# Gates of the expert mixture spread across partitions by DMA, with their chain and the row normalisation moved earlier

## The chip, the cores and the metric

The kernel runs on one core of a Trainium2 chip. The metric is the device time of one execution in microseconds; the number quoted for a kernel is the median of several executions. Engines are named as in the profile: PE is the matrix engine (PEld its weight loads), DVE the vector engine, ACT the scalar engine, POOL the GpSimd engine, and SP issues the DMAs.

## The reference

Three layers run one after the other on x of shape (4, 1024, 256), that is 4096 tokens of width 256, all in float32: a mixture-of-experts feed-forward layer, an attention block with its own small feed-forward, and the same mixture again with the same weights. The change concerns the mixture, which runs twice.

```python
def _L0_ffn_ref(x, gate_W, W1, b1, W2, b2, Ws1, bs1, Ws2, bs2, route_scale):
    scores = sigmoid(x @ gate_W) * route_scale
    topk_scores, topk_idx = top_k(scores, 2)            # 8 experts, 2 chosen
    topk_w = topk_scores / topk_scores.sum(-1, keepdims=True)
    gate_full = einsum('bsk,bske->bse', topk_w, one_hot(topk_idx, 8))
    h = gelu(einsum('bsd,edh->bseh', x, W1) + b1)
    y = einsum('bseh,ehd->bsed', h, W2) + b2
    expert_out = einsum('bse,bsed->bsd', gate_full, y)
    shared = gelu(x @ Ws1 + bs1) @ Ws2 + bs2
    return expert_out + shared

x = x + 0.5 * ffn(layernorm(x))
x = x + attention(layernorm(x))
x = x + 0.5 * ffn(layernorm(x))
```

## The kernel before

`ffn_phase` is the mixture. It is called twice: with tag `f` (first, `tail` set, which also normalises its output twice and transposes it for the attention) and with tag `g` (last, `tail` None). Tiles carry the tag: `f_gbc` and `g_gbc` are the same buffer of the two calls. Between them run `attention_phase` (tag `a`) and `mlp_phase` (tag `m`).

A call works through NB = 8 blocks of BT = 512 tokens. Within a block, `body` runs nine steps e = 0 to 8, one for the shared expert (e = 0) and one for each of the eight experts. All products use a split of each float32 operand into a rounded part and a remainder ("hi" and "lo"), so a product takes three matmuls. In a step PE does: `first_layer` (L855, 6 matmuls of 512 columns into one of two `hid` banks), then `gate` (L873, for e of 1 to 8: one matmul of 512 columns that multiplies a selector `sel` by the stack of transposed gates `gst`, and so leaves the gate of expert e for each token on all 128 partitions, in one of two `gbc` banks), then `second_layer` (L896, 12 matmuls of 256 columns into `acc`) for the step two before, e-2, so that at e = 0 and 1 it still works on the last two steps of the block before. ACT applies GELU (L469) and rounds the gated result to its hi part (L461); DVE multiplies GELU's result by the gate (`gating`, L670, one operand in PSUM) and takes the remainder (`lo`, L676). `second_layer` of step e waits for `lo` of step e; DVE does `lo` of step e during step e+1, right after `gating` of e+1.

Each engine has its own program and works in the order written in its `body`; semaphores tie them. Into the nine steps of block i the code weaves the preparation of block i+1. DVE: `x_stats` (L576, L581; mean and variance) at e = 0, `x_norm` (L594) at e = 1, `xt_lo` (L601) at e = 2, `neg_logits` (L608, L610) at e = 4, `choices` (L627 to L636; the two best experts) at e = 7, `gates` (L643 to L661; their weights, padded in `gpad`) at e = 8. PE: `transposes` (L822) at e = 2, `logits` (L832) at e = 3, and `gates_up` (L842, transposes `gpad`) of block i itself at e = 0 of block i, followed on DVE by `gate_stack` (L665, copies it to `gst`). ACT: `xt_hi` (L442) at e = 2. POOL: `x_rstd` (L536, L538), and `expneg` (L552, a power on 32 elements for each partition). In block 0 of call `f` these are two steps later (`later`). At e = 1 DVE also does `result` (L687) of block i-1. Call `f` adds for block i-1: `z_stats` at e = 3 and `zz_stats` at e = 5 on DVE, `z_rstds` on POOL, `z_norm` and `zn_norm` (L407) on ACT at e = 4 and 7, transposes of `zn` on PE at e = 8, with `zt_hi` (L449) and `zt_lo` (L718); the first and last block of `f` also split the attention's weights (`qkv_lo`, L700) and sum biases (L437, L707) on ACT and DVE.

All these transposes, logits and gates go through the two banks of one PSUM tile, `aux`. SP issues the loads and stores of rows (L330 to L366); `keep_weights` (L302 to L305) stores the split weights for call `g`.

## Time and profile before

| | us |
|---|---|
| median of 3 runs | 2463.55 |
| lowest and highest of them | 2456.26, 2467.4 |
| the profiled execution | 2457.1 |
| its span, first to last instruction | 2454.2 |
| mean granted PE clock, of full speed | 0.996 |

Call `f` takes from 0 to about 287 us of the span, call `g` from about 2196 us to the end. The page of the profile gives the engines' busy time; a busy PE is not PE at its peak, since its matmuls are pipelined and their ends are modelled. How often an engine starts something is therefore read from starts in the timeline, not from durations. "Idle before" is the time in which an engine had nothing running ahead of a group, with the operation whose end released it.

### The profile page before, as it was taken

How to read it: one execution, taken by the hardware profiler on the slowest of the kernel's cores; microseconds unless marked ns; L12 is line 12 of the kernel's file. 1: busy time of each engine (PE TensorE's matmuls, PEld its weight loads, DVE VectorE, ACT ScalarE, POOL GpSimd, SP SyncE). 2: the span in 40 equal slices, each digit the busy share in tenths (PEclk: the TensorE clock that was granted, in tenths of full speed). 3: DMA queues.
4: the chain of work that ended last, by engine and by line, in shares of the span. 5: the costliest groups of instructions: out<-in, count | busy, mean ns of one | idle time of the engine just before them, and what ended most of it. 6: DMA issues, size and time to landing. Idle time of an engine off the chain costs nothing.

```text
span 2454.2 us, 46643 instructions
## 1 busy us (share of the span) xinstructions
PE 2405.0 (98%) x14568; PEld 2087.9 (85%) x14568; DVE 1862.3 (76%) x3599; ACT 1686.6 (69%) x2920; POOL 1505.2 (61%) x1536
## 2 busy tenths in 40 slices
PE   8999889999999999999999999999999999999999
PEld 7888778888888888888888888888888879988888
DVE  7777677878878788887878878788887865556665
ACT  4555577878778787777878778787877864543333
POOL 1333277787777777767777777777768754542220
PEclk9999999999999999999999999999999999999999
DMA  5422531223212132221213312132221345331111
GB/s 204 172 102 94 181 112 44 87 68 96 95 40 89 45 101 71 75 95 43 86 60 100 97 35 94 43 98 73 77 95 43 108 169 171 122 130 34 46 51 43
DMA packets 128311, 220.16 MB, mean 90 GB/s; under 512 B 6810, under 2 KB 89652, under 8 KB 119476
## 3 DMA queue, kind: packets, MB, share of 16 engines
q1 hardware_dynamic: 128180, 218.78, 27.6%
q8 instruction: 37, 0.61, 0.1%
q14 instruction: 94, 0.77, 0.1%
HBM read 114.95 MB, written 53.48 MB: 69 GB/s over the span
## 4 chain that ended last, share of the span: by engine, by line
PE 81%; DVE 8%; issue 6%; POOL 2%; ACT 2%; DMA 1%; SPq 0%; DVEq 0%; ACTq 0%; POOLq 0%
PE a_ov L1622 19%; PE a_sc L1586 18%; PE a_tr L1598 18%; PE a_pj L1541 7%; PE a_pj L1550 4%; PE g_acc L896 3%; PE g_hid L855 3%; PE f_acc L896 3%; PE f_hid L855 2%; PE m_proj L2025 1%; POOL m_zin L1877 1%; PE m_hid L2091 1%; DVE f_hp L676 1%; DVE g_hp L676 1%; PE g_aux L832 1%
## 5 line engine op out<-in xcount | busy, mean ns | idle before, releaser
L1498 DVE TENSOR_REDUCE a_nmax<-a_sc 128x1 f32<-128x1024 f32 x512 | 626.8, 1224 | 260.3 <-PE a_sc L1586 252.1
L1425 POOL TENSOR_SCALAR a_pr<-a_pr,a_rden 128x1024 f32<-128x1024 f32 x512 | 575.1, 1125 | 256.2 <-DVE a_rden L1503 185.7
L1341 ACT ACTIVATE a_pT<-a_tr 128x512 fp32r<-128x512 f32 x1024 | 559.8, 596 | 205.5 <-PE a_tr L1598 197.2
L1509 DVE TENSOR_TENSOR a_pT<-a_tr,a_pT 128x512 fp32r<-128x512 f32 x1024 | 650.1, 677 | 17.7 <-ACT a_pT L1341 17.7
L1622 PE MATMUL a_ov<-a_pT,a_v_s 128*128 128x512 f32 x2048 | 600.2, 415 | 3.1 <-DVE a_half L1489 2.0
L1347 ACT ACTIVATE a_pr<-a_sc,a_nmax 128x1024 f32<-128x1024 f32 x512 | 573.5, 1120 | 31.8 <-DVE a_nmax L1498 28.2
L1586 PE MATMUL a_sc<-a_k_s,a_q_s 128*128 128x512 f32 x2048 | 554.1, 392 | 3.4 <-DMA a_k_s<-a_k_s 3.4
L1598 PEld LDWEIGHTS a_tr<-f_ident,a_pr 128*128 128x128 f32 x4096 | 473.0, 140 | 93.6 <-DVE a_pT L1509 18.8
L1598 PE MATMUL a_tr<-f_ident,a_pr 128*128 128x128 f32 x4096 | 537.8, 273 | 9.8 <-DVE a_pT L1509 9.6
L1586 PEld LDWEIGHTS a_sc<-a_k_s,a_q_s 128*128 128x128 f32 x2048 | 380.0, 188 | 83.7 <-DMA a_k_s<-a_k_s 3.6
L1622 PEld LDWEIGHTS a_ov<-a_pT,a_v_s 128*128 128x128 f32 x2048 | 347.5, 189 | 54.3 <-issue 4.9
L1541 PE MATMUL a_pj<-a_z_s,a_wqk_s 128*128 128x512 f32 x756 | 193.6, 391 | 2.5 <-issue 2.2
L1541 PEld LDWEIGHTS a_pj<-a_z_s,a_wqk_s 128*128 128x128 f32 x756 | 141.6, 188 | 34.9 <-issue 3.3
L1302 ACT ACTIVATE a_staged<-a_pj,f_bias 128x512 f32<-128x512 f32 x126 | 86.8, 689 | 93.8 <-PE a_pj L1541 77.4
L469 ACT ACTIVATE g_act_out<-g_hid,f_b 128x512 f32<-128x512 f32 x72 | 49.6, 688 | 144.5 <-PE g_hid L855 144.5
L896 PEld LDWEIGHTS f_acc<-f_w2p,f_hp 128*128 128x128 f32 x864 | 114.0, 193 | 11.1 <-DVE f_hp L676 6.3
L469 ACT ACTIVATE f_act_out<-f_hid,f_b 128x512 f32<-128x512 f32 x72 | 49.2, 684 | 107.0 <-PE f_hid L855 107.0
L896 PE MATMUL f_acc<-f_w2p,f_hp 128*128 128x256 f32 x864 | 117.5, 286 | 4.5 <-DVE f_hp L676 3.9
L896 PEld LDWEIGHTS g_acc<-g_w2p,g_hp 128*128 128x128 f32 x864 | 112.1, 190 | 8.2 <-DVE g_hp L676 2.9
L896 PE MATMUL g_acc<-g_w2p,g_hp 128*128 128x256 f32 x864 | 115.5, 283 | 1.3 <-DVE g_hp L676 0.9
L855 PE MATMUL f_hid<-f_xT,f_w1p 128*128 128x512 f32 x432 | 115.7, 404 | 0.0
L855 PE MATMUL g_hid<-g_xT,g_w1p 128*128 128x512 f32 x432 | 113.1, 397 | 0.0
(222 smaller groups left out, 3260.0 us busy)
## 6 DMA issues: line engine op xcount, KB each, us to landing
a_z_s<-zT SPq DMA_DIRECT2D x32, 1024.0 KB, 7.8
a_k_s<-a_k_s SPq DMA_DIRECT2D x62, 512.0 KB, 5.7
a_wqk_s<-w_split SPq DMA_DIRECT2D x64, 256.0 KB, 3.2
a_v_s<-a_v_b SPq DMA_DIRECT2D x16, 1024.0 KB, 4.6
att<-a_ao SPq DMA_DIRECT2D x32, 512.0 KB, 2.9
m_in<-att SPq DMA_DIRECT2D x16, 1024.0 KB, 6.1
a_wv_s<-w_split SPq DMA_DIRECT2D x17, 512.0 KB, 3.8
zT<-f_zT SPq DMA_DIRECT2D x8, 1024.0 KB, 3.9
```

What stands on the lines that cost most here:

```text
L469: act.activation(act_out[:, e % 3], hid[:, (par + e) % 2], ACT.Gelu, bias=b1[:, weights_of(e):weights_of(e) + 1]).then_inc(s["gelu"], 1)
L855: o = pe.matmul(hid[:, (par + e) % 2], w1p[:, a, (c * NE + x) * HID:(c * NE + x + 1) * HID], xT[:, par, c, b], start=(n == 0), stop=(n == 5))
L896: o = pe.matmul(acc[:, t], hp[:, e % 3, a, t * P:(t + 1) * P], w2p[:, b, x * D:(x + 1) * D], start=False, stop=(e == NE - 1 and (a, b) == ...
L1341: act.activation(pT[:, (u // 4) % 2, 0, 4 * part:4 * part + 4, (u % 4) * P:(u % 4 + 1) * P], tr[:, part].rearrange("p (t q) -> p t q", t=4 ...
L1347: act.activation(pr[:, k % NP], sc[:, k % 2], ACT.Exp, bias=nmax[:, k % NP:k % NP + 1], accum_out=den[:, k % NP:k % NP + 1]).then_inc(s["e ...
L1425: pool.tensor_scalar(pr[:, k % NP], pr[:, k % NP], rden[:, k % NP:k % NP + 1], 1.0, ALU.mult, ALU.mult).then_inc(s["normed"], 1)
L1498: dve.tensor_reduce(nmax[:, k % NP:k % NP + 1], sc[:, k % 2], AX.X, ALU.max, negate=True).then_inc(s["negmax"], 1)
L1509: dve.tensor_tensor(to[:, 1], tr[:, part].rearrange("p (t q) -> p t q", t=4), to[:, 0].bitcast(F32), ALU.subtract).then_inc(s["tr_lo"], 1)
L1541: o = pe.matmul(bank[:], wqk_s[:, "QK".index(kind), c, a], z_s[:, c * 2 + b, part], start=(i == 0), stop=(i == 5))
L1586: o = pe.matmul(sc[:, k % 2, kb * BT:(kb + 1) * BT], q_s[:, slot, head, tile * P:(tile + 1) * P], k_s[:, slot, head, a, kb * BT:(kb + 1) * ...
L1598: o = pe.transpose(tr[:, part, j * P:(j + 1) * P], pr[:, (k - LAG) % NP, (4 * part + j) * P:(4 * part + j + 1) * P], ident[:])
L1622: o = pe.matmul(ov[:], v_s[:, vslot, kt, 2 * vhead:2 * vhead + 2] .rearrange("p k f -> p (k f)"), pT[:, blk % 2, a, kt], start=(kt == 0 an ...
```

## The change

Blocks 0 and 1 of each call keep the `gate` matmul. For blocks 2 to 7 it is left out. Instead the exact gates are written to a third place of `gpad` (rows 64 to 71 of its transpose), ACT copies these 8 rows of 512 gates from PSUM to `gf` (`gate_copy`), SP stores them to memory (16 KB) and loads them back with one row for all partitions (`gates_across`, two DMAs of four experts each, 1 MB each, into `gB`), and `gating` reads `gB` instead of the PSUM bank. The `gbc` banks, free in these blocks, take the transposes, logits and gates of the next block (`up_bank`); `aux` keeps the `zn` transposes.

The preparation of block i+1 moves within block i to the steps in `STEADY` (before: statistics 0, normalise 1, transposes 2, logits 3, `neg` 4, `choices` 7, `gates` 8, `gates_up` and `gate_stack` at e = 0 of block i+1), and statistics and normalisation are done a block ahead, for block i+2 at e = 6 and 7. `z_stats` moves from e = 3 to 2. On POOL, `expneg` comes before `z_rstds`, and `x_rstd(i + 2)` last. Block 0 has its own schedule, `FIRST`, and does the statistics and normalisation of blocks 1 and 2. Call `f` loads `xin[:, 1]` ahead of the selector and second-layer weights. Several semaphores are merged, here and in the attention and the small feed-forward, with the same order of waits. `body` of `over_blocks` is now written out for blocks 0, 1, 6 and 7.

```diff
+    STEADY = dict(up_x=0, logits=1, neg=2, choices=3, gates=4, up_gates=6, gf=6, stack=6)
+    FIRST = dict(stats=1, norm=2, up_x=3, logits=4, neg=5, choices=7, gates=7, up_gates=8, stack=8) if tail else \
+        dict(stats=0, norm=1, up_x=2, logits=3, neg=4, choices=6, gates=7, up_gates=8, stack=8)
...
+    def on_pe(i):
+        return isinstance(i, int) and i < 2
+    def up_bank(i):
+        return aux if on_pe(i) else gbc
...
+            sp.dma_start(xin[:, 1], rows_of(src, 1)).then_inc(s["sel_in"], 16)
+            sp.wait_ge(s["padded"], 1)
...
+        def gates_across(i, counts):
+            copied, out, used = counts
+            half = E // 2
+            sp.wait_ge(s["gf"], copied)
+            sp.dma_start(gate_rows, gf[EXACT:EXACT + E]).then_inc(s["gates_out"], 16)
+            sp.wait_ge(s["gates_out"], out)
+            for h in range(2):
+                if h == 1:
+                    sp.wait_ge(s["gated"], used)
+                sp.dma_start(gB[:, h * half:(h + 1) * half].rearrange("p e t -> p (e t)"),
+                             gate_rows[h * half:(h + 1) * half].rearrange("e t -> (e t)").unsqueeze(0).partition_broadcast(P))\
+                    .then_inc(s["gates_in%d" % h], 16)
...
+        def gate_copy(i):
+            act.wait_ge(s["gT_ps"], i + 1)
+            if not on_pe(i - 1):
+                act.wait_ge(s["gates_out"], (i - 2) * 16)
+            act.activation(gf[EXACT:EXACT + E], up_bank(i - 1)[EXACT:EXACT + E, 0], ACT.Identity).then_inc(s["gf"], 1)
...
-                if e == 2 + later(first) and not last:
-                    xt_hi(i + 1, 1 - par)
+                if now("up_x", e, first) and not last:
+                    xt_hi(i + 1, 1 - par, up_bank(i))
+                if now("gf", e, first) and not last:
+                    gate_copy(i + 1)
...
-            if not last:
-                x_rstd(i + 1)
-            if tail and not first:
-                z_rstds(i - 1, 0)
+            if first:
+                x_rstd(1)
             if not last:
                 expneg(i + 1)
             if tail and not first:
+                z_rstds(i - 1, 0)
                 z_rstds(i - 1, 1)
+            if has(i, 2):
+                x_rstd(i + 2)
...
+            dve.tensor_copy(gpad[:, :, EXACT:EXACT + E], ga[:])
...
+        def gate_stack(i, par, bank):
+            if on_pe(i):
+                dve.wait_ge(s["gT_ps"], i + 1)
+            else:
+                dve.wait_ge(s["gf"], i - 1)
+            dve.tensor_copy(gst[:, par], bank[:, 0]).then_inc(s["gst"], 1)
         def gating(i, e):
             dve.wait_ge(s["gelu"], i * NE + e + 1)
-            dve.wait_ge(s["gbc"], i * E + e)
-            dve.tensor_tensor(gated[:, e % 3], gbc[:, (e - 1) % 2], act_out[:, e % 3],
-                              ALU.mult).then_inc(s["gated"], 1)
+            if on_pe(i):
+                dve.wait_ge(s["gbc"], i * E + e)
+                gate = gbc[:, (e - 1) % 2]
+            else:
+                dve.wait_ge(s["gates_in%d" % ((e - 1) // (E // 2))], (i - 1) * 16)
+                gate = gB[:, e - 1]
+            dve.tensor_tensor(gated[:, e % 3], gate, act_out[:, e % 3], ALU.mult).then_inc(s["gated"], 1)
...
+                if not last and now("neg", e, first):
+                    neg_logits(i + 1, up_bank(i))
                 if not shared(e):
                     gating(i, e)
                 if e == 1 and not first:
@@ -769,32 +830,37 @@
                     lo(i, e - 1)
                 elif e == 0 and not first:
                     lo(i - 1, NE - 1)
-                if e == 0:
-                    gate_stack(i, par)
+                if e == 0 and first:
+                    gate_stack(0, 0, aux)
                 if tail and first and e == 0:
                     qkv_bias(gbc[:, 1], 1, FIRST_BIAS)
                     w2_low(slice((NE - 1) * D, NE * D))
                 if tail and first and e == 1:
                     w2_low(slice(0, (NE - 1) * D))
                 if not last:
-                    if e == 0 + later(first):
+                    if now("stats", e, first):
                         x_stats(i + 1, 1 - par)
-                    if e == 1 + later(first):
+                    if now("norm", e, first):
                         x_norm(i + 1, 1 - par, False)
-                    if e == 2 + later(first):
-                        xt_lo(i + 1, 1 - par)
-                    if e == 4 + later(first):
-                        neg_logits(i + 1)
+                    if now("up_x", e, first):
+                        xt_lo(i + 1, 1 - par, up_bank(i))
                 if tail and not first:
-                    if e == 3:
+                    if e == 2:
                         z_stats(i - 1)
                     if e == 5:
                         zz_stats(i - 1)
                 if not last:
-                    if e == 7 + later(first) // 2:
+                    if now("choices", e, first):
                         choices(i + 1)
-                    if e == 8:
+                    if now("gates", e, first):
                         gates(i + 1)
+                if has(i, 2):
+                    if e == 6:
+                        x_stats(i + 2, par)
+                    if e == 7:
+                        x_norm(i + 2, par, False)
+                if not last and now("stack", e, first):
+                    gate_stack(i + 1, 1 - par, up_bank(i))
...
-            if shared(e):
+            if shared(e) or not on_pe(i):
...
-                if e == 0 and not first:
-                    if tail:
-                        pe.wait_ge(s["zT_lo"], (i - 1) * DC + 1)
-                    gates_up(i)
                 if not last:
-                    if e == 2 + later(first):
-                        transposes(i + 1, xn, s["xn"], s["xT_ps"])
-                    if e == 3 + later(first):
-                        logits(i + 1, 1 - par)
+                    if now("up_x", e, first):
+                        if not first:
+                            pe.wait_ge(s["gst"], i + 1)
+                        if not on_pe(i):
+                            pe.wait_ge(s["gated"], i * E)
+                            pe.wait_ge(s["gf"], i - 1)
+                        transposes(i + 1, xn, s["xn"], s["xT_ps"], up_bank(i))
+                    if now("logits", e, first):
+                        logits(i + 1, 1 - par, up_bank(i))
+                    if now("up_gates", e, first):
+                        gates_up(i + 1, up_bank(i))
                 if e == 8 and tail and not first:
-                    if not last:
-                        pe.wait_ge(s["neg"], i + 2)
+                    if on_pe(i):
+                        pe.wait_ge(s["gst"], i + 2)
+                        pe.wait_ge(s["gf"], i)
+                    pe.wait_ge(s["zT_lo"], i * DC)
                     transposes(i - 1, zn, s["zn"], s["zT_ps"])
```

## Rows read from the trace of the kernel before

**Rows 1.** Windows, call `f`: us; busy PE, PEld, DVE, ACT, POOL; PEclk, DMA share, GB/s
```profile
146.00:177.00 31.00, 30.79 (x202) 27.70 (x201) 25.24 (x83) 16.07 (x29) 9.00 (x9) 1.00 0.28 101
```

**Rows 2.** Timeline, L888 alone: the four bias matmuls at e = 2 of a block
```profile
L888 PE MATMUL f_acc<-f_b2s,f_gst x4: 278/282/282, 25.0 to 25.3; 128*128 128x256 f32 x4
...
L888 PE MATMUL f_acc<-f_b2s,f_gst x4: 274/280/282, 61.9 to 62.2; 128*128 128x256 f32 x4
...
L888 PE MATMUL f_acc<-f_b2s,f_gst x4: 277/280/354, 158.9 to 159.3; 128*128 128x256 f32 x4
...
L888 PE MATMUL f_acc<-f_b2s,f_gst x4: 278/281/354, 191.4 to 191.8; 128*128 128x256 f32 x4
...
L888 PE MATMUL g_acc<-f_b2s,g_gst x4: 278/281/283, 2298.6 to 2299.0; 128*128 128x256 f32 x4
...
L888 PE MATMUL g_acc<-f_b2s,g_gst x4: 278/281/283, 2330.3 to 2330.6; 128*128 128x256 f32 x4
```

**Rows 3.** Timeline, one step (e = 7) of a block of `g`: start, us, engine, line
```profile
2315.56 1.24 PEld L855 LDWEIGHTS g_hid<-g_xT,g_w1p 128*128 128x128 f32 x6
...
2316.84 0.19 PEld L873 LDWEIGHTS g_gbc<-g_gst,g_sel 128*128 128x128 f32 x1
...
2317.07 1.61 PEld L896 LDWEIGHTS g_acc<-g_w2p,g_hp 128*128 128x128 f32 x12
...
2318.08 0.69 DVE L670 TENSOR_TENSOR g_gated<-g_gbc,g_act_out 128x512 f32<-128x512 f32 x1 [1.76 <-ACT g_act_out L469]
...
2318.61 1.24 PEld L855 LDWEIGHTS g_hid<-g_xT,g_w1p 128*128 128x128 f32 x6
...
2318.68 0.68 DVE L676 TENSOR_TENSOR g_hp<-g_gated,g_hp 128x512 fp32r<-128x512 f32 x1
```

**Rows 4.** Timeline, the same block: start and end of `choices` and `gates`
```profile
2319.28 0.17 DVE L627 TENSOR_SCALAR g_sg<-g_nl 128x32 f32<-128x32 f32 x1
...
2321.64 0.69 DVE L670 TENSOR_TENSOR g_gated<-g_gbc,g_act_out 128x512 f32<-128x512 f32 x1 [0.21 <-DVE g_idx L636]
...
2325.00 0.69 DVE L676 TENSOR_TENSOR g_hp<-g_gated,g_hp 128x512 fp32r<-128x512 f32 x1
...
2325.14 0.42 PEld L842 LDWEIGHTS g_aux<-f_ident,g_gpad 128*128 128x128 f32 x4 [0.59 <-DVE g_gpad L661]
```

**Rows 5.** DVE by line and form, one block of `f`: busy us, mean ns
```profile
L576 DVE BATCH_NORM_STATS2 f_zst<-f_zz 128x6 f32<-128x256 f32 x4 | 1.4, 412 | 0.0
...
L594 DVE TENSOR_SCALAR f_xn<-f_xin,f_mv,f_rs 128x256 f32<-128x256 f32 x4 | 1.4, 406 | 0.0
```

**Rows 6.** Timeline of `f`: POOL operations and the DVE operations beside them
```profile
138.54 5.43 POOL L552 TENSOR_TENSOR f_nl<-f_ebase,f_nl 128x32 f32<-128x32 f32 x1 [1.22 <-DVE f_nl L610]
...
140.82 0.68 DVE L676 TENSOR_TENSOR f_hp<-f_gated,f_hp 128x512 fp32r<-128x512 f32 x1
...
143.85 0.68 DVE L676 TENSOR_TENSOR f_hp<-f_gated,f_hp 128x512 fp32r<-128x512 f32 x1
...
144.05 0.54 POOL L535 TENSOR_SCALAR f_zshift<-f_zmv 128x4 f32<-128x4 f32 x1
```

**Rows 7.** Timeline, ends of blocks 0 and 7 of `f`
```profile
52.78 0.66 PE L842 MATMUL f_aux<-f_ident,f_gpad 128*128 128x128 f32 x4 [1.99 <-DVE f_gpad L661]
...
57.04 2.77 PE L896 MATMUL f_acc<-f_w2p,f_hp 128*128 128x256 f32 x12
...
266.22 2.08 ACT L407 ACTIVATE f_zz<-f_res,f_zshift,f_zrs 128x256 f32<-128x256 f32 x4 [2.01 <-POOL f_zshift L548]
...
271.91 2.38 PE L896 MATMUL f_acc<-f_w2p,f_hp 128*128 128x256 f32 x12 [2.63 <-DVE f_hp L676]
```

**Rows 8.** DMA issues: KB each, median us from issue to landing
```profile
a_z_s<-zT SPq DMA_DIRECT2D x32, 1024.0 KB, 7.8
...
zT<-f_zT SPq DMA_DIRECT2D x8, 1024.0 KB, 3.9
...
f_iota<-in_iota SPq DMA_DIRECT2D x1, 4.0 KB, 2.9
```

More of the change, by code:

```diff
@@ L175, in ffn_phase @@
         b2_in = m.sb("b2_in", [P, D], room=rooms.wide)
-        xres = m.sb("xres", [P, NT, D], room=rooms.rows)
+        xres = m.sb("xres", [P, NT, D], room=rooms.wide)
+        gB = m.sb("gB", [P, E, BT], room=rooms.rows)
+        gf = m.sb("gf", [P, BT], room=Rooms().loads)
         res = m.sb("res", [P, NT, D], room=rooms.tail)
@@ L232, in ffn_phase @@
     names = ("veps x_in xres bn stats rstd xn xT_ps xT_hi xT_lo logits neg expneg "
-             "gate gpad gT_ps gst hid gelu gbc gated h_hi h_lo out res res_out padded")
+             "gate gpad gT_ps gst hid gelu gbc gated h_hi h_lo out res res_out padded "
+             "gf gates_out gates_in0 gates_in1")
     if tail:
-        names += " gate_in w1_in w2_in zeroed gw_hi w1_hi w2_hi sel gw_lo w1_lo w2_lo b2_hi b2_stack kept"
+        names += " gate_in w1_in w2_in gw_hi w_hi rounded gw_lo w_lo b2_stack kept"
         names += " z_veps z_bn z_stats z_rs z_rstd z zn zT_ps zT_hi zT_lo zT_out z_out qkv_in v_in sel_in scaled summed qs qkv_hi qkv_lo qkv_out bias_ps bias"
@@ L258, in ffn_phase, with now, has @@
     SUMS_AT = {4: 0, 6: 1, 7: 2}
-    def later(first):
-        return 2 if tail and first else 0
+    STEADY = dict(up_x=0, logits=1, neg=2, choices=3, gates=4, up_gates=6, gf=6, stack=6)
+    FIRST = dict(stats=1, norm=2, up_x=3, logits=4, neg=5, choices=7, gates=7, up_gates=8, stack=8) if tail else \
+        dict(stats=0, norm=1, up_x=2, logits=3, neg=4, choices=6, gates=7, up_gates=8, stack=8)
+    def now(what, e, first):
+        return (FIRST if first else STEADY).get(what) == e
+    def has(i, ahead=0):
+        return not isinstance(i, int) or 0 <= i + ahead < NB
+    def on_pe(i):
+        return isinstance(i, int) and i < 2
+    def up_bank(i):
+        return aux if on_pe(i) else gbc
     def over_blocks(eng, body):
         body(0, 0, True, False)
-        with eng.Fori(0, (NB - 2) // 2) as it:
-            body(it * 2 + 1, 1, False, False)
+        body(1, 1, False, False)
+        with eng.Fori(0, (NB - 4) // 2) as it:
             body(it * 2 + 2, 0, False, False)
+            body(it * 2 + 3, 1, False, False)
+        body(NB - 2, 0, False, False)
         body(NB - 1, 1, False, True)
@@ L319, in rows_ahead @@
             sp.dma_start(xin[:, 0], rows_of(src, 0)).then_inc(s["x_in"], 16)
-        def has(i, ahead=0):
-            return not isinstance(i, int) or 0 <= i + ahead < NB
         def fixed(i):
@@ L342, in store_z @@
             sp.dma_start(to, zz[:]).then_inc(s["z_out"], 16)
+        def gates_across(i, counts):
[10 more added lines that the diff above has]
+                    .then_inc(s["gates_in%d" % h], 16)
         def body(i, par):
+            if has(i, 1) and not (isinstance(i, int) and i == 0):
+                counts = [fixed(n) for n in (i, i * 16, i * E + E)]
             if has(i, 2):
@@ L368, in body @@
                 store_z(i - 1, z_to)
+            if has(i, 1) and not (isinstance(i, int) and i == 0):
+                gates_across(i, counts)
         def store_qkv(k):
@@ L584, in x_stats @@
         def x_stats(i, par):
-            dve.wait_ge(s["x_in"], i * 16 + 16)
+            if tail and isinstance(i, int) and i == 1:
+                dve.wait_ge(s["sel_in"], 80)
+            else:
+                dve.wait_ge(s["x_in"], (i - 1) * 16 + 16 if tail and not (isinstance(i, int) and i == 0) else i * 16 + 16)
             norm_stats(xin[:, par], st6, mv, s["bn"], s["stats"], i + 1)
@@ L837, in logits, with gates_up @@
             o.then_inc(s["logits"], 1)
[L839 removed]
+        def gates_up(i, bank=aux):
             pe.wait_ge(s["gpad"], i + 1)
             for t in range(NT):
[L842 removed]
+                o = pe.transpose(bank[:, 0, t * P:(t + 1) * P], gpad[:, t], ident[:])
             o.then_inc(s["gT_ps"], 1)
```

95 lines of the change are left out of this document (46 added, 49 removed).

## The prediction

> **What bounds the kernel now.** I looked first at the busy time by stretch, then at the starts in the timeline of one block. In a block of call `f` PE has something in flight for 30.79 of 31 us, DVE for 25.24, ACT for 16.07, POOL for 9.00 [rows 1]. So PE's own issue is the bound and DVE is next, with 81% of the stretch. The starts give PE's price list [rows 3]: six matmuls of `first_layer` take 2316.84 - 2315.56 = 1.28 us, the gate matmul 2317.07 - 2316.84 = 0.23, twelve of `second_layer` 2318.61 - 2317.07 = 1.54; a step is 3.05. The gate matmul lasts 0.39 but takes a slot of only 0.23, since the next starts before it ends. From one group of bias matmuls to the next, a block takes 191.4 - 158.9 = 32.5 us in `f` and 2330.3 - 2298.6 = 31.7 in `g` [rows 2].
>
> PE is not without holes. At the end of a block DVE does `choices` (2321.64 - 2319.28 less 0.21 idle = 2.15) and, one step on, `gates` (2325.00 - 2321.64, less 1.20 for `gating` and `lo`, = 2.16), and `gates_up` then finds its input late: PE's loads stand still for 0.59 [rows 4]. `gating` and `lo` take 0.60 each from start to start [rows 3, 4].
>
> **How near DVE runs to PE.** This decides the case. In the undisturbed step `gating` starts 2.52 us after `first_layer`, and the `lo` behind it ends 2318.68 + 0.68 - 2315.56 = 3.80 after it [rows 3]. `second_layer` wants that `lo` one step and one `first_layer` later: before at 3.05 + 1.28 + 0.23 = 4.56, after the change, with both gate slots gone, at 2.82 + 1.28 = 4.10. The slack falls from 0.76 to 0.30. Whatever DVE does in a step beyond PE's length for that step adds to a lag, and a lag over 0.30 is a wait on PE.
>
> **Part 1: the gate matmuls.** 8 x 6 x 2 = 96 go. At 0.23 each that is 22.1 us of PE, all of it on the path. Nothing takes their place on PE: the transposes, logits and `gates_up` are as many as before.
>
> **Part 2: the late gates.** `gates_up` now comes at e = 6, over a step and a half after `gates` at e = 4, so the 0.59 [rows 4] goes. `result` at e = 1 now has the logits of PE beside it and no normalisation behind it, so a short wait of PE there, which I put at 0.2, goes too. Together 0.8 us a block; `f`, whose period is that of `g` plus eight transposes, has about as much.
>
> **Part 3: what is late next.** DVE's work by step after the change, against PE's 2.82 plus what is woven in. `choices` and `gates` now follow each other at e = 3 and 4: 1.20 + 2.15 and 1.20 + 2.16 + 0.1 (one more small copy) against 2.82 each, 1.17 too much, so in `g` 1.17 - 0.30 = 0.9 us of new waits a block. In `f`, statistics of 1.4 + 0.4 us [rows 5] stand at e = 2 (with `neg`, 0.4; PE has 0.5 of bias matmuls) and at e = 5 (+0.2), and at e = 6 there are statistics for the block after next and `gate_stack` (as one `lo`, 0.60), 3.6 against 3.2. The chain e = 2 to 6 sums to 2.0 too much; less 0.30, 1.7 of new waits. After e = 6 PE has its transposes and logits and DVE catches up. So a block comes to -1.84 - 0.8 + 0.9 = -1.75 in `g`, and -1.84 - 0.8 + 1.6 = -1.0 in `f`. I take 1.6 for `f`, since waits also slow what feeds DVE.
>
> **Part 4: the DMA.** Each block stores 16 KB and loads 2 x 1 MB. The first half must be there for `gating` at e = 1 of the next block. PE does from `gate_copy` to there the rest of e = 6, e = 7, 8 and 0, and one `first_layer` and GELU: some 11.5 us in `g`, 12.5 in `f`, where eight more transposes lie between. The trace shows no such load. The nearest rows are 2.9 us for a tiny load and 3.9 and 7.8 for 1 MB [rows 8]; the sum is 2.9 + 3.9 = 6.8 to 2.9 + 7.8 = 10.7, plus two issues of 0.4. Both ends fit, the upper just. I take nothing, and below a broadcast of which each us too many costs 1 us a block. SP issues these last in its `body`, when its queue is empty; behind the second half, which waits for `gated` of e = 8, stand the next block's stores, which nobody waits for, and in `f` `keep_weights`, which moves behind the end of block 1. The rows of block 4 are queued behind it and are wanted at e = 6 of block 2, some 20 us later; I count no wait.
>
> The Trainium skill, in "SBUF — State Buffer", section "Who interferes with whom", speaks against the change: DVE and GpSimd share a read interface, a DVE instruction with two SBUF inputs contends with a GpSimd instruction that reads SBUF, and the later one waits for all of the other. `gating` becomes such an instruction 96 times. The trace agrees one way: POOL's small operation at 144.05 takes 0.54 and ends just behind the `lo` that began at 143.85 and ended at 144.53 [rows 6]. It disagrees the other way: the `lo` at 140.82 reads two SBUF tiles in the middle of POOL's 5.43 us power and takes its usual 0.68 [rows 6].
>
> So I price `gating` from SBUF as `lo`, 0.68 against 0.69 from PSUM [rows 3], and POOL's chain gets a delay of up to 0.5 for each operation that meets one.
>
> **Part 5: POOL's power.** It takes 5.43 [rows 6] and starts, after `neg`, some 0.7 us after the logits, so its result is there 6.2 after them. `choices` at e = 3 comes at 2.82 + 0.5 (e = 2) + 3.7 (up to the end of `lo`) = 7.0. Before, there were three steps between them; the margin is now 0.8. `z_norm` in `f` waits for POOL's z work behind the power, which ends about 8.1 after the logits, against 9.2 when ACT comes to it.
>
> **Part 6: the ends of the calls.** Start of `f`: half a MB of rows goes ahead of the selector and weights in a full queue. By the difference of a tiny load and 1 MB, halved, that is (3.9 - 2.9) / 2 = 0.5 to (7.8 - 2.9) / 2 = 2.5 us [rows 8]; I take 1.3, and the gates of block 0 follow the weights: +1.3. Block 0 of `f` took 61.9 - 25.0 = 36.9 us [rows 2]: PE waited 1.99 for `gates_up` [rows 7] and more for `gst`, and the clock then fell, so that twelve matmuls took 2.77 instead of 1.6 [rows 7, 3]. After the change `choices`, `gates` and a normalisation of 1.4 [rows 5] all stand at e = 7: the wait at `gates_up` stays about 2.1; the second wait shrinks to 0.9, because the weight splits no longer lie ahead of `gate_stack`; and x statistics ahead of `lo` of e = 1 cost 1.3. I leave half of the clock's loss: -0.8. Block 1 is -0.2. Block 6 lacks the statistics for a block 8: another -0.7. In block 7 ACT waited 2.01 for POOL, and PE then 2.63, again followed by slow matmuls (2.38 for twelve) [rows 7]; with `z_stats` a step earlier and no power in front of it, `z_norm` finds its input, and a wait of some 1.3 from ACT's own work is left: -2.7, and -1.3 for its gate slots. In `g`, block 0 does two blocks' statistics and normalisations beside `choices` and `gates` at e = 6 and 7: 5.2 + 4.9 us of DVE against 2 x 3.05. That is 3.0 of waits where there were 0.6: +2.4. Block 1 of `g` -0.9, block 7 -1.3. The attention and its feed-forward between the calls keep their order: 0.
>
> **The sum.** `f`: +1.3 - 0.8 - 0.2 - 5 x 1.0 - 0.7 - 1.3 - 2.7 = -9.4. `g`: +2.4 - 0.9 - 5 x 1.75 - 1.3 = -8.55. Together -18. The profiled execution took 2457.1, so it would be 2439.1. The median of the runs shown is 6.4 above it; predicted time 2463.55 - 18 = 2445.5.
>
> **The rivals.**
> - A: no new waits. If DVE's lag never reaches PE, because in the trace slack is larger than I count, the waits of part 3 are not there: 5 x (1.6 + 0.9) = 12.5 less, 2433. For it: the old `gates` step was as dense, and PE lost only 0.59. Against it: that step had eight or four matmuls and a step without `gating` behind it. 0.10.
> - B: the power meets `choices`. If POOL is 1 us later than in part 5, because `gating` now blocks its reads, DVE waits ahead of `gating` of e = 4, and each block loses 1 us; 12 blocks, 2457.5. For it: the margin of 0.8 and the 0.54 for 0.2 of rows 6. Against it: the power itself always took 5.43. 0.23.
> - C, on the other side: the broadcast is late. All 128 rows read the same 8 KB, which no row here does. With 16 us from `gate_copy` to landing, `g` waits 4.4 and `f` 2.8 a block, in five blocks each: +36, 2481.5. It decides from about 14 us, where it eats up the gain. 0.11.
> - D: DVE is shut out by POOL's power, so that one `gating` a block waits for most of 5.43 us: 12 x 4 = +48, 2493. Rows 6 speak against it. 0.04.
>
> The forecast itself has 0.52. Its own range is 2437 to 2455, by the spread of the runs (±5) and of block 0 (±3).
>
> **How the numbers follow.** The range reaches to A's time and over B's: 2432 to 2464. It leaves out C, D and the far side of A. A measurement of this kernel can tell 0.5%, 12 us, from no change. Faster by more than that: most of the forecast, 0.47, A, 0.10, and a little of B, 0.03, together 0.60. Within it: the rest of the forecast, 0.05, most of B, 0.20, and a C that just eats the gain, 0.02: 0.27. Slower: 0.13.
>
> **What would show it.** The period of a block between bias matmuls: 31.5 in `f` and 30.0 in `g`, from block 2 on. No wait of PE for `gpad` in these blocks, and waits of 0.3 to 0.9 for `hp` at e = 5, 6 and, in `f`, 8. `gated` out of `gB` at 0.68. DVE not idle in front of `gated` of e = 1; if it is, with a DMA as releaser, C holds. If DVE idles in front of `sg` for POOL, B. At the end of block 0 of `f` a wait for `gpad` of about 2, in block 7 none of ACT for `zshift`. What would make it wrong most: a lag of DVE that runs on over a block's end, or PE's clock falling after waits in block 0 of `g`.

## The result, and the profile after

| | before | after |
|---|---|---|
| median of 10 runs each, us | 2464.48 (2455.8 to 2467.4) | 2446.64 (2438.0 to 2453.1) |
| ratio, 95% interval | | 0.9933 (0.9918 to 0.9947) |
| span of the profiled execution, us | 2454.2 | 2438.9 |
| matmuls in the trace | 14568 | 14472 |

The change makes the kernel faster by 0.7%. The forecast was 2445.5. From the page of after, first busy time and instructions, then the new DMAs (KB each, median us to landing):

```profile
span 2438.9 us, 46253 instructions
...
PE 2382.4 (98%) x14472; PEld 2066.2 (85%) x14472; DVE 1865.4 (76%) x3615; ACT 1693.0 (69%) x2932; POOL 1512.4 (62%) x1536
...
f_gB<-f_gate_rows SPq DMA_DIRECT2D x12, 1024.0 KB, 5.0
g_gB<-g_gate_rows SPq DMA_DIRECT2D x12, 1024.0 KB, 4.7
```

The 96 gate matmuls are gone. The answers to [rows 2] are the bias matmuls of after, now L955 (count: min/median/max ns, first and last start):

```profile
L955 PE MATMUL f_acc<-f_b2s,f_gst x4: 278/283/283, 26.6 to 26.9; 128*128 128x256 f32 x4
...
L955 PE MATMUL f_acc<-f_b2s,f_gst x4: 277/282/283, 64.8 to 65.1; 128*128 128x256 f32 x4
...
L955 PE MATMUL f_acc<-f_b2s,f_gst x4: 277/282/283, 128.0 to 128.3; 128*128 128x256 f32 x4
...
L955 PE MATMUL f_acc<-f_b2s,f_gst x4: 277/282/283, 159.6 to 160.0; 128*128 128x256 f32 x4
...
L955 PE MATMUL g_acc<-f_b2s,g_gst x4: 278/280/280, 2196.2 to 2196.6; 128*128 128x256 f32 x4
...
L955 PE MATMUL g_acc<-f_b2s,g_gst x4: 278/283/283, 2234.2 to 2234.6; 128*128 128x256 f32 x4
...
L955 PE MATMUL g_acc<-f_b2s,g_gst x4: 278/283/283, 2294.4 to 2294.7; 128*128 128x256 f32 x4
...
L955 PE MATMUL g_acc<-f_b2s,g_gst x4: 278/283/283, 2324.3 to 2324.6; 128*128 128x256 f32 x4
```

A block of `f` takes 159.6 - 128.0 = 31.6 us (32.5 before, [rows 2]), one of `g` 2324.3 - 2294.4 = 29.9 (31.7). The table has the same reading for every kernel of this document: "steady" is the period of blocks 2 to 5, each from its own bias matmuls to those of the next block (starts are read to 0.1 us, so a period can be off by 0.1); "block 0" is the interval from the first bias matmul to the second; "middle" runs from the last of `f` to the first of `g`, nearly all of it attention; "late" says whether ScalarE's late `a_pT`, found further down, is there. The ratio is to before, timed on the same chip.

| kernel | steady `f` | steady `g` | block 0 `f`, `g` | middle | late | ratio (95%) |
|---|---|---|---|---|---|---|
| before | 32.5 | 31.7 | 36.9, 32.7 | 1946.2 | yes | 1 |
| after | 31.4-31.9 | 29.9 | 38.2, 38.0 | 1945.7 | yes | 0.9933 (0.9918-0.9947) |
| after_again | 31.4-31.7 | 29.9 | 38.2, 38.0 | 1945.9 | yes | 0.9932 (0.9914-0.9951) |
| gate_twice | 33.6 | 32.8 | 36.5, 33.6 | 1953.2 | yes | 1.0088 (1.0068-1.0108) |
| schedule_only | 32.0-32.2 | 30.8 | 38.2, 38.0 | 1942.2 | no | 0.9935 (0.9916-0.9955) |
| schedule_only_again | 32.0-32.3 | 30.8 | 38.2, 37.9 | 1937.1 | no | 0.9931 (0.9909-0.9953) |
| schedule_only_shifted | 32.0-32.3 | 30.9 | 38.3, 38.0 | 1949.1 | yes | 0.9970 (0.9957-0.9984) |
| dve_at_4 | 31.9-32.0 | 30.4-30.5 | 38.2, 37.7 | 1949.5 | yes | 0.9967 (0.9952-0.9983) |
| dve_at_0 | 31.3-32.0 | 29.9 | 39.1, 37.7 | 1951.4 | yes | 0.9925 (0.9909-0.9942) |
| store_seven_times | 32.0-33.5, once 40.0 | 33.3-34.0 | 38.2, 38.0 | 1945.1 | yes | one execution: 2485.4 |
| ends | 31.4-31.9 | 29.9 | 36.8, 35.1 | 1948.7 | yes | 0.9920 (0.9894-0.9947) |
| spread_chain | 30.6 | 29.1 | 36.7, 35.2 | 1951.6 | yes | 0.9881 (0.9859-0.9903) |
| gates_on_TensorE_spread | 31.7 | 30.8 | 36.8, 35.1 | 1938.8 | no | 0.9882 (0.9863-0.9902) |
| spread_chain_shifted | 30.6 | 29.1 | 36.8, 35.2 | 1931.9 | no | 0.9838 (0.9816-0.9859) |

One reading needs care. In after the next block's transposes and logits come at e = 0 and 1, ahead of the bias matmul, where they came behind it. A step of 2.82 us with transposes is 0.8 to 0.9 longer and one with logits 1.79, so about 2.7 us move into block 0's interval and out of the last one. Like for like, after's block 0 is 35.5 in `f` and 35.3 in `g`.

The waits of after from block 1 of `g` to its end (2232 to 2440), and then in blocks 1 to 7 of `f` (62 to 260); us in total, times, longest:

```profile
DVE g_gated L730 <- ACT g_act_out L514: 44.7, 42, 2.4
DVE g_hp L735 <- ACT g_hp L506: 13.0, 7, 2.4
PEld g_acc L963 <- DVE g_hp L735: 7.3, 12, 0.9
```
```profile
PEld f_acc L963 <- DVE f_hp L735: 10.9, 17, 0.8
```

DVE never waits for `gB`, so the broadcast is in time. The wait for `gpad` of [rows 4] is gone. What is left is PE's weight loads on `hp`, which is `lo` coming late: the new wait that was forecast. Part of it lies behind running matmuls; PE itself stands still 0.3 to 0.4 at a time in the steady blocks. The timeline of one block of `g` shows the chain from the gates to their use (start, us, engine, line): the store, the two loads, and the first `gating` of the next block:

```profile
2309.86 0.29 SPq L368 DMA_DIRECT2D g_gate_rows<-g_gf  x1
2311.31 3.81 SPq L374 DMA_DIRECT2D g_gB<-g_gate_rows  x2
...
2320.76 0.69 DVE L730 TENSOR_TENSOR g_gated<-g_gB,g_act_out 128x512 f32<-128x512 f32 x1 [0.80 <-ACT g_act_out L514]
```

Store and wait take 2311.31 - 2309.86 = 1.45 us, by the median of the landings the first load is there 4.7 later, at 2316.0, and it is wanted at 2320.76: 4.7 us to spare.

### The profile page after: what moved, and what is told of

The parts are those of the page before. It is cut to its first block, busy times and chain, and to the rows that moved or that the text cites. A ratio compares the mean times of both kernels' runs of the same rounds, so it can differ in the third digit from the quotient of the medians.

```text
span 2438.9 us, 46253 instructions
## 1 busy us (share of the span) xinstructions
PE 2382.4 (98%) x14472; PEld 2066.2 (85%) x14472; DVE 1865.4 (76%) x3615; ACT 1693.0 (69%) x2932; POOL 1512.4 (62%) x1536
## 3 DMA queue, kind: packets, MB, share of 16 engines
q1 hardware_dynamic: 131828, 244.15, 30.8%
## 4 chain that ended last, share of the span: by engine, by line
PE 81%; DVE 8%; issue 5%; POOL 2%; ACT 2%; DMA 1%; SPq 0%; DVEq 0%; ACTq 0%; POOLq 0%
PE a_ov L1693 19%; PE a_sc L1657 18%; PE a_tr L1669 18%; PE a_pj L1612 7%; PE a_pj L1621 4%; PE g_acc L963 3%; PE g_hid L921 3%; PE f_acc L963 2%; PE f_hid L921 2%; PE m_proj L2096 1%; POOL m_zin L1948 1%; PE m_hid L2162 1%; DVE f_hp L735 1%; DVE f_gated L730 1%; DVE a_pT L1580 1%
## 5 line engine op out<-in xcount | busy, mean ns | idle before, releaser
L1418 ACT ACTIVATE a_pr<-a_sc,a_nmax 128x1024 f32<-128x1024 f32 x512 | 573.7, 1120 | 32.8 <-DVE a_nmax L1569 29.3
L1612 PEld LDWEIGHTS a_pj<-a_z_s,a_wqk_s 128*128 128x128 f32 x756 | 142.3, 189 | 35.5 <-issue 3.4
L514 ACT ACTIVATE f_act_out<-f_hid,f_b 128x512 f32<-128x512 f32 x72 | 49.2, 685 | 93.3 <-PE f_hid L921 93.3
```

The source lines that it names most:

```text
L514: act.activation(act_out[:, e % 3], hid[:, (par + e) % 2], ACT.Gelu, bias=b1[:, weights_of(e):weights_of(e) + 1]).then_inc(s["gelu"], 1)
L1418: act.activation(pr[:, k % NP], sc[:, k % 2], ACT.Exp, bias=nmax[:, k % NP:k % NP + 1], accum_out=den[:, k % NP:k % NP + 1]).then_inc(s["e ...
L1612: o = pe.matmul(bank[:], wqk_s[:, "QK".index(kind), c, a], z_s[:, c * 2 + b, part], start=(i == 0), stop=(i == 5))
```

## The experiments

**What a gate matmul costs.** The kernel before, with each gate matmul issued twice.

```diff
-            pe.matmul(gbc[:, (e - 1) % 2], sel[...], gst[:, par], start=True, stop=True).then_inc(s["gbc"], 1)
+            for _ in range(2):
+                o = pe.matmul(gbc[:, (e - 1) % 2], sel[...], gst[:, par], start=True, stop=True)
+            o.then_inc(s["gbc"], 1)
```

> The kernel before with each of its 128 gate matmuls issued twice into the same bank. If a gate matmul is worth its issue slot of 0.23 us and PE is the bound, 128 x 0.23 = 29.4 us more than before, a block 1.84 longer in both calls (34.3 in f, 33.5 in g). If DVE's pace sets the blocks (rival), PE has room and it is under 10 us more. If the price is the duration of 0.39, it is 50 us more.

Measured: 1.0088, and periods 33.6 and 32.8, so 8 more slots cost 1.1 us a block, not 1.84. The rest went into waits that before has anyway: in the steady blocks of `g` PE's loads stand still for 0.59 and 0.28 a block in before, and never in gate_twice. A slot on PE is worth 0.23 only while PE waits for nothing. That is the first sign that removed slots, too, may buy less than their length.

**The schedule without the DMA.** After, but the gates of every block come from PE; no `gate_copy`, no `gates_across` (two waits of PE are adapted as well, not shown).

```diff
     def on_pe(i):
-        return isinstance(i, int) and i < 2
+        return True
...
-                if now("gf", e, first) and not last:
-                    gate_copy(i + 1)
...
-            if has(i, 1) and not (isinstance(i, int) and i == 0):
-                gates_across(i, counts)
```

> The kernel after with its new schedule, but the gate matmuls kept on PE in all blocks and no gates sent by DMA (all through the old PSUM banks, with the waits that this needs). Theory: PE gets 1.84 us a block back, and the slack between DVE and PE grows from 0.30 to 0.76, so 0.46 of the new waits goes: 1.4 more than after a block, 33.0 in f and 31.3 in g, in all some 16 us over after, about the time of before. The schedule alone then gains nothing. Rival: the gain of the change comes from the earlier gates (no wait at gates_up), and this stays within 8 us of after.

Measured: 0.9935, as fast as after. The periods, 32.0 to 32.2 and 30.8, are longer than after's and shorter than before's. The number in the expectation was reckoned wrongly: with steps of 3.05 each step's overhang shrinks by 0.23 too (in `g` 1.17 - 0.46 = 0.7, under the slack of 0.76), so there is no wait left to add, and in `g` 30.8 is PE's bare work (its loads wait 0.25 once a block, PE itself not at all). That PE is free of waits in `g` is what the theory of the lag says. That the kernel is as fast as after is not, since its mixture takes some 9 us more; it is settled further down.

**Is it DVE's lag at e = 3 to 6?** After, with one DVE operation of 0.60 us more in each of the blocks 1 to 6, at e = 4 or, in the control, at e = 0. Its result is used by nothing.

```diff
+                if e == 4 and not first and not last:    # dve_at_0: e == 0
+                    dve.tensor_tensor(spare[:], w2p[:, 0, 0:BT].bitcast(F32), w2p[:, 0, BT:2 * BT].bitcast(F32), ALU.subtract)
```

> The kernel after with one more DVE subtraction of 128x512 (0.60 us from start to start) at the end of e = 4 in blocks 1 to 6 of both calls. Theory (DVE's lag in e = 3 to 6 is what PE waits for): each block of 2 to 6 is 0.60 longer, 32.2 in f and 30.5 in g, 6 to 7 us in all. Rival (PE's own issue is the bound, the waits for hp are latency): no change.

> The same operation at the end of e = 0 instead, where DVE has time to spare. Theory: no change to after, within 0.1 us a block. Rival (DVE's total load sets the block): 0.60 a block longer here too.

Measured: at e = 4 the periods grow by 0.6 in `g`, so there a DVE operation of 0.60 lies on the path one for one. In `f` they grow by 0.1 to 0.5, block against block, so part of it is swallowed. At e = 0 they stay as they are (31.3 to 31.4 in all but one block of `f`, 29.9); only the interval of block 0 of `f`, which holds e = 0 of block 1, grew, by 0.9. DVE is busy the same in both; only the place differs. So DVE's share of the block does not bound it. The lag at the dense steps does.

**Repeats.** after_again and schedule_only_again are the same two kernels once more, with more runs.

> The kernel after itself, unchanged, for a comparison with the others of this call on one chip: some 16 us under before, blocks of 31.5 us in f and 29.9 in g.

> Schedule alone, gates on PE, once more beside after. From the periods already seen (32.1 and 30.9 against 31.5 and 29.9) the mixture parts should cost 5 x 0.6 + 6 x 1.0 = 9 us more than after, so some 7 to 9 us under before. The first run of it came out as fast as after, with PE in the attention busy 99.96 us of 100 instead of 99.6. If the new code puts the attention into that better rhythm, it stays level with after; if that was chance, it falls behind by 7 to 9.

Measured: 0.9932 and 0.9931. From first to last bias matmul the two calls together are 9 us shorter in after, both times. The middle part is shorter in schedule_only, by 3.6 us in the first pair and 8.8 in the second (the first execution of schedule_only lost 7 us elsewhere in the attention; see the last section). The attention's code is the same. Neither theory has a place for that.

**Where the lateness of the broadcast would begin.** After, with the store of the gates done and waited for seven times.

```diff
-            sp.dma_start(gate_rows, gf[EXACT:EXACT + E]).then_inc(s["gates_out"], 16)
-            sp.wait_ge(s["gates_out"], out)
+            for out in outs:                              # seven values
+                sp.dma_start(gate_rows, gf[EXACT:EXACT + E]).then_inc(s["gates_out"], 16)
+                sp.wait_ge(s["gates_out"], out)
```

> After, with the gates' 16 KB stored to memory seven times over, each store waited for, before they are loaded back across the partitions. In the run of after one store and its wait took 1.45 us and the first half of the gates had landed 4.7 us before its first gating in g, so six more put it 6 x 1.45 = 8.7 us later and 4.0 us too late there. If the transfer's margin is what keeps it free of cost: DVE waits some 4 us at the gating of expert 1, the lag swallows 0.5 to 1 of it, periods g 29.9 -> about 33.2 and f 31.5 -> about 34 in the blocks with gates by DMA, in all +30 to +40 us. If the broadcast's cost were bandwidth or contention and not its lateness: periods unchanged, since the six stores move 96 KB only.

Measured: 2485.4 in one execution, some 40 us over after. The wait that the forecast named for rival C is there, in `g` (from 2232 to the end) and then in `f` (62 to 260):

```profile
DVE g_gated L732 <- DMA g_gB<-g_gate_rows: 31.7, 6, 6.7
```
```profile
DVE f_gated L732 <- DMA f_gB<-f_gate_rows: 13.6, 5, 3.3
```

That is 5.3 us a block in `g` and 2.7 in `f`; the periods grow by 3.4 to 4.1 in `g` and by up to 2.0 in `f`. The load itself landed in 5.8 us here instead of 4.7, so it came 8.7 + 1.1 - 4.7 = 5.1 late by the margin read in after: the margin is real. One block of `f` (97.3 to 137.3, 40.0 us) lost much more. SyncE had issued the stores of `keep_weights` at 92 to 93 us, its next load of rows then took 11.9 us to issue instead of 0.4, the seven stores behind it 13.0 instead of 9.0, and DVE waited 4.6 for `xin`. That the stores of weights held up the rest is likely, but no run shows it.

**The ends of the calls.** After, with block 0's second statistics at e = 4 and normalisation at e = 8 (before: 6 and 7), `choices` of `f`'s block 0 at e = 6, and the bias sums of block 7 at e = 2, 3 and 6.

```diff
-    SUMS_AT = {4: 0, 6: 1, 7: 2}
+    SUMS_AT = {2: 0, 3: 1, 6: 2}
-    FIRST = dict(..., choices=7, gates=7, up_gates=8, stack=8) if tail else dict(..., choices=6, gates=7, ...)
+    FIRST = dict(..., choices=6, gates=7, up_gates=8, stack=8, stats2=4, norm2=8) if tail else dict(..., stats2=4, norm2=8)
```

> The kernel after with three moves at the ends: statistics of block 2 in block 0 at e = 4 and its normalisation at e = 8 behind gate_stack, choices of block 1 in f at e = 6, and in block 7 of f the three bias products on ACT at e = 2, 3, 6 instead of 4, 6, 7. Theory: in g PE's waits of 1.30, 0.55 and 0.44 in block 0 go (period 38.0 to about 35.5), in f the 1.83 for gpad (38.2 to about 36.2), and the waits of 1.60 and 2.41 in block 7 of f shrink to under 1 and 1.3. Sum about 7 us under after. Rival (block 7 waits for POOL's normalisation, not for ACT's load): the last two stay.

Measured: block 0 took 36.8 instead of 38.2 and 35.1 instead of 38.0. In block 7 of `f` both waits of PE shrank as expected, while ScalarE still waits for POOL (timeline of ends):

```profile
255.73 1.69 PE L964 MATMUL f_acc<-f_w2p,f_hp 128*128 128x256 f32 x12 [0.71 <-DVE f_hp L735]
...
266.60 2.08 ACT L445 ACTIVATE f_zn<-f_zz,f_zshift,f_zrs 128x256 f32<-128x256 f32 x4 [0.90 <-POOL f_zshift L595]
...
270.64 3.50 PE L964 MATMUL f_acc<-f_w2p,f_hp 128*128 128x256 f32 x24 [0.75 <-DVE f_hp L735]
```

From the last bias matmul of `f` to the attention's first matmul it is 25.6 us instead of 28.0 in after_again. So the intervals give back 1.4 + 2.9 + 2.4 = 6.7 us of the 7 expected. The profiled span is only 1.9 us shorter, since this execution spent 6.9 us more at the start of the attention (last section), and the timed ratio, 0.9920 (0.9894 to 0.9947), is too wide to tell 7 us.

**Spreading the chain.** ends, with `choices` and `gates` cut in four parts over more steps, so that no step is as dense as before.

```diff
-    STEADY = dict(up_x=0, logits=1, neg=2, choices=3, gates=4, up_gates=6, gf=6, stack=6, stats2=6, norm2=7)
+    STEADY = dict(up_x=0, logits=1, neg=2, choices=3, places=4, weights=4, gates=6, up_gates=7, gf=7, stack=7, stats2=7, norm2=8) if tail else \
+        dict(up_x=0, logits=1, neg=2, choices=3, places=4, weights=4, gates=5, up_gates=6, gf=6, stack=6, stats2=6, norm2=7)
```

> As ends, and the gates' chain spread over more steps: in g choices up to the maxima at e = 3, places and weights at e = 4, the rest at e = 5; in f the rest at e = 6, gates_up, gate_copy and gate_stack at e = 7, statistics at 7 and normalisation at 8. No DVE work is added or removed. Lag theory: g 29.9 to 29.0 us a block and f 31.5 to about 30.2, 11 us less than ends. Rival (total DVE work): as ends.

Measured: 0.9881, periods 30.6 and 29.1, and PE's waits in the steady blocks of `g` gone (its loads still wait 0.28 once a block). Same work, 1.0 us a block less in `f` and 0.8 in `g`: that was the price of density.

**The DMA against PE once nobody waits.** spread_chain, with the gates of all blocks from PE (the edit of schedule_only).

> The kernel spread_chain with the gates of all blocks spread by TensorE instead of by DMA. If after's small gain from the DMA part (0.6 us a block in f, 1.0 in g, against slots of 1.84) is due to waits that DVE's chain put in, those waits are gone here in both kernels and the DMA part is worth its slots: f 30.6 + 1.6 to 1.84 = 32.2 to 32.4, g 29.05 + 1.84 = 30.9, mixture about 20 us longer than spread_chain's. If the DMA part itself costs something: less than 1.5 us a block. Attention has been 9 us shorter in kernels with this ScalarE stream, so in all about 2436 to 2440.

Measured: periods 31.7 and 30.8. In `g` the DMA part is now worth 1.7 us a block, nearly all of 8 x 0.23 = 1.84. In `f` it is 1.1, and the weight loads of spread_chain account for the rest, 0.8 a block: over its blocks 2 to 4 (94.2 to 186) they still wait for `lo`, where the kernel with PE's gates has no such line.

```profile
PEld f_acc L980 <- DVE f_hp L743: 2.5, 6, 0.4
```

From the first bias matmul to the last, `f` is 6.3 us shorter and `g` 9.1 with the DMA. And yet both kernels have the same ratio, 0.9881 and 0.9882. Again the attention, whose middle part is 12.8 us longer in spread_chain, takes it back.

**What happens in the attention.** TensorE is busy 996.0 of 1000 us from 700 to 1700 in after and 999.6 in schedule_only. ScalarE's timelines differ in one place: once every 105.3 us ScalarE stands idle for 2.0 us ahead of an `a_pT`, where 0.5 to 0.8 is usual and 0.77 is what schedule_only shows in the same place of the round. The expectations further down call this "2.0 us after its matmuls", which is not what the row says: all eight matmuls that feed it end at 722.44 + 1.04 = 723.48, 0.9 us before it begins. In after:

```profile
722.44 1.04 PE L1669 MATMUL a_tr<-f_ident,a_pr 128*128 128x128 f32 x8
...
724.36 1.09 ACT L1412 ACTIVATE a_pT<-a_tr 128x512 fp32r<-128x512 f32 x2 [2.04 <-PE a_tr L1669]
...
829.65 1.09 ACT L1412 ACTIVATE a_pT<-a_tr 128x512 fp32r<-128x512 f32 x2 [2.01 <-PE a_tr L1669]
...
935.00 1.09 ACT L1412 ACTIVATE a_pT<-a_tr 128x512 fp32r<-128x512 f32 x2 [1.99 <-PE a_tr L1669]
```

Its input was there, nothing stood ahead of it on ScalarE, and all of DVE and PE behind it slipped. It is in before, in gate_twice and in every kernel so far that has the DMA, once in each round of attention's loop, and neither in the two runs of schedule_only nor in gates_on_TensorE_spread. What differs for ScalarE is that these lack the instructions of `gate_copy`: attention's loop begins at instruction 499 of ScalarE's compiled program there, in after at 508. So I moved the loop and nothing else, with waits on a semaphore that has long been there:

```diff
             act.sem_inc(s["zT_out"], 16)
+            for _ in range(19):                    # compiled to 9 instructions; spread_chain_shifted: range(111), 55
+                act.wait_ge(s["z_out"], 16)
             act.preload_act_table(ACT.Exp)
```

> schedule_only with 9 instructions more in ScalarE's stream, waits on a semaphore that is already there, at its very start; attention's loop then begins at instruction 508 of ScalarE's stream as in after, and not at 499. If attention's late a_pT of ScalarE (2.0 us after its matmuls once in 105.3 us in before, after and five more kernels, never in the two runs of schedule_only) hangs on where the loop lies in ScalarE's stream: it is back, TensorE is busy 996 of 1000 us from 700 to 1700, the middle part 1946 us, in all 9 us more, about 2448. If it hangs on anything else that differs (PE's, DVE's or SyncE's stream, the order of the DMAs): 999.7 of 1000, middle part 1937, 2440.

> spread_chain with 55 instructions more at the start of ScalarE's stream, where it waits for the first loads anyway; attention's loop then begins at instruction 563 = 499 + 64, a shift of schedule_only's place by a multiple of 64. If the late a_pT hangs on the loop's place in ScalarE's stream, modulo some power of two up to 64: it is gone, the middle part falls from 1952 to about 1942 and the time from 2428 to about 2419. If the place is not what decides, or it counts otherwise: as spread_chain, 2428.

Measured: schedule_only_shifted 0.9970, against 0.9935 and 0.9931 without the nine instructions, with the same periods in the mixture. ScalarE's waits and the busy time of 700 to 1700 (columns as in [rows 1]) of schedule_only:

```profile
ACT a_pT L1408 <- PE a_tr L1665: 118.2, 228, 0.8
```
```profile
700.00:1700.00 1000.00, 999.61 (x5821) 854.82 (x5820) 813.91 (x1337) 801.23 (x1415) 765.56 (x792) 1.00 0.24 74
```

and of schedule_only_shifted:

```profile
ACT a_pT L1410 <- PE a_tr L1667: 119.3, 215, 2.1
```
```profile
700.00:1700.00 1000.00, 995.30 (x5769) 846.60 (x5768) 807.27 (x1324) 793.55 (x1402) 759.09 (x784) 1.00 0.24 74
```

The late `a_pT` is back, and 52 matmuls fewer fit in the stretch. The other way round, spread_chain_shifted starts the loop at 563 = 499 + 64: there the delay is gone (999.62 of 1000) and the kernel takes 2415.56 us, 0.9838 of before, the fastest here. From the first matmul that reads `a_pT` to the last, the kernels with the delay need 1667 to 1671 us and those without 1656 to 1662.

So the delay hangs on where the loop lies in ScalarE's program. Of the four places seen, 399 (before) and 508 have it, 499 and 563 don't. The traces also show where in the round it begins: right behind the loop's own branch. Of after and then schedule_only, the branch and the next instruction of ScalarE's sequencer (count: min/median/max ns, first and last start):

```profile
L1188 ACTq COMPARE_BRANCH  x1: 45/45/45, 721.8 to 721.8; - x1
...
L1188 ACTq FUSED_REGOPS  x1: 68/68/68, 724.2 to 724.2; - x1
```
```profile
L1184 ACTq COMPARE_BRANCH  x1: 45/45/45, 732.2 to 732.2; - x1
...
L1184 ACTq FUSED_REGOPS  x1: 68/68/68, 732.4 to 732.4; - x1
```

In all ten rows of the table with the delay the next instruction comes 2.3 to 2.8 us after the branch, each of the 13 times that the loop goes round; in the four without it, 0.2 us. So it is ScalarE's sequencer that stands still, and the late `a_pT` is the first work behind it. That it waits for its instructions there would fit, but no row shows what it waits for; which places are good in general is open.

## Why the prediction was right, and where it was not

*The sum.* Medians fell by 17.8 against 18 forecast, with an interval of 13 to 20. The profiled span fell by 15.3: `f` by 7.85 (9.4 forecast), `g` by 9.0 (8.55), and what lies between them grew by 1.6 (0). That the median came so near is in part luck.

*Part 1.* The slots are gone. They are worth 1.7 us a block in `g` where PE does not wait. Against schedule_only_shifted, which has the same schedule and the same attention, after gains 0.9933 / 0.9970 = 0.37%, 9 us of the 22.1 (give or take 5, by the intervals of the two ratios), and the schedule alone the other 0.3%; the mixture's intervals say the same for the slots (9.2 us between after_again and schedule_only_again). The rest became waits for DVE, as part 3 had it.

*Parts 2 and 3.* Periods 31.5 and 30.0 forecast, 31.4 to 31.9 and 29.9 measured; waits for `hp` at e = 5, 6 and, in `f`, 8, none for `gpad`. dve_at_4 and dve_at_0 show the lag itself, and spread_chain that undoing it brings back 0.8 us in `g`, near the 0.9 priced in; for `f` 1.6 were priced in and 1.0 found by spreading, which leaves 0.8 a block of weight loads waiting.

*Part 4.* Store, wait and load took 1.45 + 4.7 = 6.2 us of 10.9 in `g`, below the lower bound of 6.8. After, its repeat and the five other kernels that load `gB` once show no wait for it, and the one made late does. Rival C was a matter of 5 us, not of the mechanism: decided "at about 14 us", it set in at 6.2 + 4.7 = 10.9 in `g`.

*Part 5.* POOL's power takes 5.43 as before and ends 0.5 us ahead of `choices` (0.8 was forecast). One block of `g`, POOL and DVE beside it:

```profile
2293.90 5.43 POOL L599 TENSOR_TENSOR g_nl<-f_ebase,g_nl 128x32 f32<-128x32 f32 x1 [11.69 <-DVE g_nl L661]
```
```profile
2295.32 0.69 DVE L730 TENSOR_TENSOR g_gated<-g_gB,g_act_out 128x512 f32<-128x512 f32 x1 [1.50 <-ACT g_act_out L514]
...
2299.83 0.17 DVE L678 TENSOR_SCALAR g_sg<-g_nl 128x32 f32<-128x32 f32 x1
```

The power ends at 2299.33 and DVE, which first finishes its `lo`, does not wait. The `gating` from SBUF at 2295.32 runs inside the power in 0.69. So neither B nor D came. By the Trainium skill, "SBUF — State Buffer", section "Who interferes with whom", the later of two such instructions waits for the whole of the other; the trace doesn't show that for this power: none of the 48 `gating` from `gB` in `g` takes more than 0.695, and all eight powers of `g` have a mean of 5.43.

*Part 6, start and block 0 of `f`.* +1.6 (forecast +1.3) and, like for like, 35.5 against 36.9 = -1.4 (-0.8). PE did wait 1.83 for `gpad` (2.1 forecast), 0.44 behind it (0.9), and 1.04 + 0.56 after the statistics (1.3), but the clock that was granted stayed at full speed over block 0 (mean 1.00 from 28 to 65; before 0.90 from 28 to 62), where half of the old loss had been left in. Blocks 1 to 6 bring it to -5.8 at the last bias matmul, with -5.4 forecast.

*Part 6, block 7 of `f`: the mis-sized term.* -4.0 were forecast, -2.7 of it because `z_norm` would find its input. It was -2.0. Timeline of after, the second half of that block (columns as in [rows 7]):

```profile
258.65 2.08 ACT L445 ACTIVATE f_zz<-f_res,f_zshift,f_zrs 128x256 f32<-128x256 f32 x4 [0.30 <-POOL f_zshift L595]
260.64 1.14 ACT L475 ACTIVATE f_qkv_in<-f_qkv_in,f_ln 128x1024 f32<-128x1024 f32 x1
...
264.35 1.70 PE L963 MATMUL f_acc<-f_w2p,f_hp 128*128 128x256 f32 x12 [1.60 <-DVE f_hp L735]
...
267.49 1.92 POOL L585 TENSOR_TENSOR f_zrs<-f_zrs,f_mhalf 128x4 f32<-128x4 f32 x1
...
269.81 2.08 ACT L445 ACTIVATE f_zn<-f_zz,f_zshift,f_zrs 128x256 f32<-128x256 f32 x4 [1.12 <-POOL f_zshift L595]
271.80 1.14 ACT L475 ACTIVATE f_qkv_in<-f_qkv_in,f_ln 128x1024 f32<-128x1024 f32 x1
...
275.51 1.22 PE L963 MATMUL f_acc<-f_w2p,f_hp 128*128 128x256 f32 x8 [2.41 <-DVE f_hp L735]
```

The first wait behaved: ACT waits 0.30 where it waited 2.01, and PE 1.60 where 1.3 were left for it. The step that failed is that it looked at this one wait. `zn_norm` has another, 1.12 for a POOL operation stretched to 1.92, and a bias product of 1.14 behind it, and PE waits 2.41, where it waited 1.24 before (at 283.35). So the first wait gave back 1.0 us and the second took 1.2. The run ends shows which of the two it was: with the bias products moved away PE waits 0.75 there, though ScalarE still waits 0.90 for a POOL operation that took 1.99. ScalarE's bias products made most of it. What the block did gain fits its gate slots (1.3 forecast) and a granted clock of 1.00 (250.5 to 278.8) instead of 0.94 (before, 256 to 287); how the two share it no run shows.

*Part 6, `g`.* Block 0 cost +2.6 (+2.4), the last interval fell as forecast, and all of `g` came to -9.0 (-8.55). In `f` it was -7.85 at attention's first matmul (-9.4).

*The attention, priced at nothing.* Nearly right for this pair (+1.6), by luck: both kernels have the late `a_pT`. A kernel whose ScalarE program has another length may gain or lose 10 us, which is more than half of what was forecast for the whole change. It had no place among the rivals.

## What to carry over

Give a removed slot of the bound engine its price only after you have added up, step by step, how far the next engine runs behind; then move that engine's work out of its dense steps first, which brought 1.0 and 0.8 us a block here and made the DMA worth 1.7 in `g` instead of 1.0. When two kernels differ in time by more than the edited stage does, compare the untouched stages too: moving a loop by a few instructions was worth 10 us here, and without the shifted kernels it would have been booked as "the DMA part brings nothing".
